# Block-scaled MLP stage: which engine multiplies by the inverse maxima, which adds the residual, and the order of TensorE's queue

## Chip, cores and metric

The kernel runs on one core of a Trainium2 chip. The metric is the device time of one execution in microseconds (us), as the median of several runs. Engines are named as the profile names them: PE (TensorE, matrix products; PEld its weight loads), DVE (VectorE), ACT (ScalarE), POOL (GpSimd) and SP (SyncE, which here only issues DMAs).

## What is computed

Two blocks, each an attention and a feed-forward part, on x of shape 32 x 64 x 128. The change touches only the last part, a gated MLP whose operands are quantized to FP4 in blocks of 16 along the last dimension:

```python
def fp4_quant_dequant(x):
    xb = x.reshape(shape[:-1] + (shape[-1] // 16, 16))
    scale = jnp.maximum(jnp.max(jnp.abs(xb), axis=-1, keepdims=True) / 6.0, 1e-12)
    xn = xb / scale
    idx = jnp.searchsorted(_MID, jnp.abs(xn))        # nearest of 0, .5, 1, 1.5, 2, 3, 4, 6
    return (_GRID[idx] * jnp.sign(xn) * scale).reshape(shape)

gate = fp4_linear(x, w_gate)          # 128 -> 352, both operands quantized
y    = fp4_linear(x, w_up)            # 128 -> 352
h    = silu(gate) * y
out  = residual + g * fp4_linear(h, w_down)   # 352 -> 128
```

## The kernel before, in words

The 2048 tokens are 16 tiles of 128 tokens. The MLP works on pairs of tiles: `PAIRS` is 8, `WHOLE` is 6 (pairs 0 to 5 are handled whole), and the last two pairs are finished in `LAST` = 4 halves. There is no planner: every engine's order is written out by hand, and each engine runs its own queue in that order. A `wait_ge` holds up everything behind it in the same queue.

For one pair q of h the steps are these.

- PE `gate(q)` and `up(q)` multiply the quantized x by the two weights into PSUM (L1599). ACT `silu(q)` (L721) writes silu(gate) to `sg`.
- DVE `pair_step(q)`: the product h = silu * up into `hh` (L1090, one input in PSUM), the maximum of each block of 16 into `hmx` (L1095, 44 maxima for each token row), their reciprocals `hin` (L1101), and `fp4_shrunk` (L286), which multiplies h in place by a constant and by the reciprocal of its block, spread over the 16 elements. That is 128 x 704 elements, and it counts `hv_done`.
- ACT `magnitude(q)` (L728) writes |h| times a constant to `hm`. DVE rounds in two steps (`fp4_off`, L294, both inputs in SBUF) into `hd`. In the queue this stands in `pair_step(q+1)`, right behind L286 of pair q+1, so it is the pair before that is rounded.
- POOL `h_scale(q)` (L290) turns the maxima into scales, and `fp4_unscale` (L301) multiplies `hd` by them, 128 x 704, into `hq`. For the last four halves DVE does this itself (`round_half`, L301 on 128 x 352).
- PE `turn_h(q)` transposes `hq` (L1625), ACT copies the result to `hT` (L775), PE `down(q)` multiplies by the down weights (L1636). `down` first adds the residual on PE, as a product of the identity with x (L1631), and ACT `finish(q)` copies the sum into x (L755) and counts `x4_done`. SP stores the pair.

The x of the MLP is quantized in the same way, in four groups of four tiles: `x_scale` (L281, L282, L286) and `x_round` (L294) on DVE, `x_unscale` (L290, L301 on 128 x 512) on POOL. Groups 2 and 3 of these stand between the steps of pairs 0 to 3.

PE's order for iteration q of the loop is `up(q+1)`, `turn_h(q-2)`, `down(q-2)`, `gate(q+2)`. ACT's is `silu(q+1)`, `finish(q-3)`, the copy of `hT` for pair q-2, `magnitude(q)`.

Of the kernel before, what the change touches and what calls it, by code (L numbers as in the profile page):

```python
# [15 lines left out]
ALU = mybir.AluOpType  # L16
# [10 lines left out]
MT = 3  # L27
# [75 lines left out]
def build(nc, a):  # L103
    with ExitStack() as ctx:
# [21 lines left out]
        def carve(start, *shape):  # L126
            return shaped(region[:, start:start + int(np.prod(shape))], shape)
# [62 lines left out]
        hb = [carve(8576 + 2 * NH * (BLK + 1) * i, 2 * NH, BLK + 1) for i in range(2)]  # L190
        xb = carve(21952, TILES * D // BLK, BLK + 1)
        hm, hd = ([carve(k + 2 * MLP * i, 2 * MLP) for i in range(2)] for k in range(12 * MLP, 20 * MLP, 4 * MLP))
        hT = [carve(7040 + 2 * MT * P * i, 2, MT, P) for i in range(2)]

        stats, mv, ve, rstd = sm(TILES, 6), sm(TILES, 2), sm(TILES), sm(TILES)
# [26 lines left out]
        x2_tr x2_done xn_c xn_c_late xn_c_dve xf_done xf_used q_done pp_done hs_done hs_read hs_turned cf_ready corr_done corr_read  # L222
        dve_c lead_ready lead_exp lags_ready lags_turned gx_ready g_done of_done of_ready
        y1_done y1_ready o_done x3_read x3_done
        floors_set hsc_ready xsc_ready rolled_made codes_set xn_d xv_done xm_done xd_done xq_done xqt_done xqt_used gate_done gu_done sg_done hh_done hv_done hm_done hd_done hq_done hq_last ht_done ht_used dn_done x4_done out_done dve_d""".split()
        m = {n: ctx.enter_context(nc.semaphore(n)) for n in names}
        x_sem = [m["ld_x0"], m["ld_x1"]]
        w_sem = [m[f"w{i}"] for i in range(6)]
# [55 lines left out]
        def fp4_shrunk(eng, out, src, inv):  # L284

            return eng.scalar_tensor_tensor(out, src, 6.0 / FINE * (1.0 - 2.0 ** -24), inv, ALU.mult, ALU.mult)  # L286
# [13 lines left out]
        def fp4_unscale(eng, diff, sc, nblk, out):  # L300
            return eng.tensor_tensor(blocks(out), blocks(diff), spread(sc, nblk), ALU.mult)  # L301


        @block.sync
        def _(sp):
            xs = a["x"].rearrange("(t u) s d -> (u s) t d", u=2)
            sp.dma_start(par[:, 0:NPAR_K], a["par"][:, 0:NPAR_K]).then_inc(m["ld_wk"], 16)
            sp.dma_start(ctxS[:, 0:8 * S], a["ctxT"][:, 0:8 * S]).then_inc(m["ld_ctx0"], 16)
            sp.dma_start(par[:, NPAR_K:NPAR_A], a["par"][:, NPAR_K:NPAR_A]).then_inc(m["ld_par"], 16)
            sp.dma_start(ctxS[:, 8 * S:16 * S], a["ctxT"][:, 8 * S:16 * S]).then_inc(m["ld_ctx1"], 16)  # L310
            sp.dma_start(x[:, 0:TILES // 2, :], xs[:, 0:TILES // 2, :]).then_inc(m["ld_x0"], 16)
            sp.dma_start(ctxS[:, 16 * S:B * S], a["ctxT"][:, 16 * S:B * S]).then_inc(m["ld_ctx2"], 16)
            sp.dma_start(x[:, TILES // 2:TILES, :], xs[:, TILES // 2:TILES, :]).then_inc(m["ld_x1"], 16)
            sp.dma_start(par[:, NPAR_A:NPAR], a["par"][:, NPAR_A:NPAR]).then_inc(m["ld_rest"], 16)
            sp.dma_start(ctxN[:], a["ctx"].rearrange("(t u) s d -> (u s) t d", u=2)).then_inc(m["ld_ctxn"], 16)
            for e in range(E):
                sp.dma_start(wall[:, e, :], a["wall"][e]).then_inc(m["ld_wall"], 16)
            sp.wait_ge(m["x1_done"], TILES)
            sp.dma_start(wnat, a["ffn"]).then_inc(m["ld_ffn"], 16)
            sp.wait_ge(m["ld_wall"], 16 * E)  # L320
            sp.wait_ge(m["experts_ready"], 1)

            def feed(j):

                e = sp.value_load(experts[0:1, j:j + 1], min_val=0, max_val=E - 1)
                if j >= 6:
                    sp.wait_ge(m["y2_done"], j - 5)
                sp.dma_start(wbuf[j % 6], wall[:, bass.ds(e, 1), :].rearrange("p a w -> p (a w)")).then_inc(w_sem[j % 6], 16)

            for j in range(MOE_TILES):  # L330
                feed(j)
            out = a["out"].rearrange("(q t u) s d -> q (u s) t d", t=2, u=2)
            for q in range(WHOLE):
                sp.wait_ge(m["x4_done"], q + 1)
                sp.dma_start(out[q], x[:, 2 * q:2 * q + 2, :]).then_inc(m["out_done"], 16)
            for n in range(LAST):
                sp.wait_ge(m["x4_done"], WHOLE + n + 1)
                q, t = WHOLE + n // 2, n % 2
                sp.dma_start(out[q][:, t:t + 1, :], x[:, 2 * q + t:2 * q + t + 1, :]).then_inc(m["out_done"], 16)
            sp.wait_ge(m["out_done"], 16 * (WHOLE + LAST))  # L340
# [3 lines left out]
        def _(pool):  # L344
# [142 lines left out]
            x_unscale(1)  # L487
            def h_scale(q):

                pool.wait_ge(m["hv_done"], q + 1)  # L490
                if q >= 3:
                    pool.wait_ge(m["hq_done"], q - 2)
                fp4_scale(pool, hmx[q % 3], hsc[q % 3]).then_inc(m["hsc_ready"], 1)

            for q in range(1, WHOLE + 1):
                u = (q - 1) % 2
                if q in (1, 3):
                    x_unscale((q + 3) // 2)
                h_scale(q - 1)
                pool.wait_ge(m["hd_done"], q)  # L500
                pool.wait_ge(m["hsc_ready"], q)
                if q >= 3:
                    pool.wait_ge(m["ht_done"], q - 2)
                fp4_unscale(pool, hd[u], hsc[(q - 1) % 3], 2 * NH, hq[u].rearrange("p a n -> p (a n)")).then_inc(m["hq_done"], 1)
            for q in range(WHOLE, PAIRS):
                h_scale(q)


        @block.scalar
        def _(act):  # L510
# [241 lines left out]
            normalise(act, 12, 16, m["xn_d"], 14, blocked=True)  # L752
            def finish(q):
                act.wait_ge(m["dn_done"], q + 1)
                act.copy(x[:, 2 * q:2 * q + 2, :].rearrange("p t d -> p (t d)"), ps[:, 7, 0:2 * D]).then_inc(m["x4_done"], 1)  # L755

            def half_turned(n):
                p, t = WHOLE + n // 2, n % 2
# [2 lines left out]

            def half_finish(n):
                act.wait_ge(m["dn_done"], WHOLE + n + 1)
                act.copy(x[:, 2 * WHOLE + n, :], ps[:, 1 + n, 0:D]).then_inc(m["x4_done"], 1)

            for q in range(PAIRS):
                if q + 1 < PAIRS:
# [23 lines left out]
        def _(dve):  # L791
# [291 lines left out]
            def pair_step(q):  # L1083

                u, w, n3 = q % 2, (q - 1) % 2, q % 3
                if q < PAIRS:
                    dve.wait_ge(m["sg_done"], q + 1)
                    dve.wait_ge(m["gu_done"], q + 1)
                    rows = "p a (n k) -> p a n k"
                    dve.tensor_tensor(hh[u].rearrange("p (a n) k -> p a n k", a=2), sg[u].rearrange(rows, k=BLK),  # L1090
                                      ps[:, 3:5, 0:MLP].rearrange(rows, k=BLK), ALU.mult).then_inc(m["hh_done"], 1)
                    if q >= 3:
                        dve.wait_ge(m["hq_done"], q - 2)
                    dve.wait_ge(m["hh_done"], q + 1)
                    k = dd.mark(dve.tensor_reduce(hmx[n3], hb[u], AX, ALU.max, apply_absolute_value=True))  # L1095
                    if q in (1, 3):
                        x_round((q + 3) // 2)
                    if q == 2:
                        x_scale(3)
                    dd.after(k)  # L1100
                    dd.step(dve.reciprocal(hin[n3], hmx[n3]))  # L1101
                    fp4_shrunk(dve, hh[u], hh[u], spread(hin[n3], 2 * NH)).then_inc(m["hv_done"], 1)
                    if q == 0:
                        x_scale(2)
                if 1 <= q <= WHOLE:
                    dve.wait_ge(m["hm_done"], q)
                    if q >= 3:
                        dve.wait_ge(m["hq_done"], q - 2)
                    dd.step(fp4_off(dve, blocks(hd[w]), blocks(hm[w]), hh[w]))
                    fp4_off(dve, hd[w], hm[w], hd[w]).then_inc(m["hd_done"], 1)  # L1110
# [29 lines left out]
        def _(pe):  # L1140
# [486 lines left out]

            def down(q):
                if q:
                    pe.wait_ge(m["x4_done"], q)  # L1630
                mm(ps[:, 7, 0:2 * D], ident, x[:, 2 * q:2 * q + 2, :].rearrange("p t d -> p (t d)"), start=True, stop=False)  # L1631
                pe.wait_ge(m["ht_used"], q + 1)
                for t in range(2):
                    for k in range(MT):
                        n = min(P, MLP - P * k)
                        ins = mm(ps[:, 7, D * t:D * t + D], hT[q % 2][0:n, t, k, :], wdT[0:n, k, :],  # L1636
                             start=False, stop=(t == 1 and k == MT - 1))
                ins.then_inc(m["dn_done"], 1)

            def turn_half(n):  # L1640
# [26 lines left out]
            for q in range(PAIRS):  # L1667
                if q + 1 < PAIRS:
                    up(q + 1)
                if q >= 2:  # L1670
                    turn_h(q - 2)
                    down(q - 2)
                if q == 0:
                    turn_x(1)
                if q + 2 < PAIRS:
                    gate(q + 2)
                if q in (1, 3):
                    turn_x((q + 3) // 2)
            turn_half(0)
# [121 lines left out]
```

## Time and profile before

| | us |
|---|---|
| median of 3 runs | 275.0 (274.87 to 275.17) |
| profiled execution, first to last instruction | 274.8 |
| MLP pair steps on DVE (L1090 of pair 0 to the last L301) | 221.16 to 270.44 |
| behind the last DVE instruction | 4.4 |

All times below are counted from the span's start. A row of a timeline has the start, the duration, the engine, the line, the operation, what it writes and reads, shapes, and "xN" where N like instructions are merged; in brackets stands how long the engine was idle before it and what ended that. An instruction's duration includes the time for which it is held up after its start, so a duration above the usual one of the same shape shows that something stood in its way. On DVE an instruction can start a little before the one ahead of it has ended.

### The profile page before, as it was taken

The numbers are of one execution on the slowest core, as the hardware profiler recorded it, in microseconds if no ns is written. First come the engines' busy times: TensorE is split into PE (matmuls) and PEld (weight loads), VectorE is DVE, ScalarE is ACT, GpSimd is POOL, SyncE is SP. The second block draws the span as 40 slices with busy tenths as digits, with TensorE's granted clock in tenths as the row PEclk, the third lists the DMA queues.
The fourth block names the chain that finished last, engine by engine and source line by source line (L and its number), as shares of the span: only waits on it lengthen the run. The fifth ranks groups of instructions, "written<-read, shape, count | busy, mean of one in ns | idle before, by whom it ended". The sixth has DMA issues, their size and how long they took to land.

```text
span 274.8 us, 6251 instructions
## 1 busy us (share of the span) xinstructions
PE 253.9 (92%) x2152; PEld 196.4 (71%) x2152; DVE 190.7 (69%) x494; ACT 164.6 (60%) x384; POOL 131.0 (48%) x207
## 2 busy tenths in 40 slices
PE   8999999999899989999999999979998784989886
PEld 6655376666577868999999999665785442766675
DVE  3898688888988763253222223885769989999993
ACT  2369985666488654675566667473445793354453
POOL 4566579999402403218992220275066633353230
PEclk9999999999999998999999999999999999799999
DMA  6999000000000209776777771000000000000111
GB/s 191 379 348 403 13 4 2 2 4 0 2 2 4 76 20 377 300 289 265 296 300 291 292 290 63 2 1 1 4 0 0 0 0 2 0 19 23 38 39 38
DMA packets 12191, 30.11 MB, mean 110 GB/s; under 512 B 1024, under 2 KB 5248, under 8 KB 12032
## 3 DMA queue, kind: packets, MB, share of 16 engines
q1 hardware_dynamic: 12160, 29.71, 28.5%
q8 instruction: 17, 0.28, 0.4%
q14 instruction: 14, 0.11, 0.1%
HBM read 9.71 MB, written 1.05 MB: 39 GB/s over the span
## 4 chain that ended last, share of the span: by engine, by line
PE 64%; DVE 20%; issue 7%; ACT 5%; POOL 2%; DVEq 0%; POOLq 0%
PE ps L1403 12%; PE ps L1414 12%; PE ps L1252 6%; DVE s_region L294 4%; PE ps L1226 4%; PE ps L1239 4%; PE ps L1159 3%; DVE s_region L1090 3%; PE ps L1542 3%; PE ps L1150 2%; DVE s_small L1095 2%; PE ps L1262 2%; PE ps L1151 2%; PE ps L1344 2%; DVE s_small L237 2%
## 5 line engine op out<-in xcount | busy, mean ns | idle before, releaser
L631 ACT ACTIVATE s_region<-ps,s_region 128x128 f32<-128x128 f32 x144 | 40.8, 371 | 21.8 <-PE ps L1403 21.8
L960 DVE SCALAR_TENSOR_TENSOR s_ctxT<-ps,s_region,s_ctxT 128x64 f32 x72 | 18.1, 281 | 43.8 <-PE ps L1414 43.8
L1403 PE MATMUL ps<-s_region 128*128 128x128 f32 x288 | 38.0, 276 | 0.3 <-issue 0.3
L1414 PE MATMUL ps<-s_region 128*128 128x128 f32 x288 | 37.9, 275 | 0.0
L1403 PEld LDWEIGHTS ps<-s_region 128*128 128x128 f32 x288 | 34.9, 192 | 0.7 <-issue 0.7
L1414 PEld LDWEIGHTS ps<-s_region 128*128 128x128 f32 x288 | 35.0, 192 | 0.2 <-issue 0.2
L420 POOL COPY s_region<-s_xt 128x64 f32 x72 | 14.8, 234 | 32.3 <-PE ps L1403 24.5
L574 ACT COPY s_region<-ps 128x512 f32<-128x512 f32 x32 | 17.2, 592 | 16.2 <-PE ps L1239 16.2
L830 DVE TENSOR_REDUCE s_small<-ps 128x16 f32<-128x1024 f32 x16 | 19.6, 1224 | 9.7 <-PE ps L1226 9.7
L1599 PE MATMUL ps<-s_region 128*128 128x352 f32 x64 | 21.1, 469 | 5.3 <-DVE s_region L1090 3.7
L301 POOL TENSOR_TENSOR s_region<-s_region,s_small 128x704 f32<-128x704 f32 (+2 forms) x11 | 14.6, 1330 | 22.0 <-DVE s_region L294 21.7
L364 POOL TENSOR_SCALAR s_region<-s_region 128x512 f32<-128x512 f32 x16 | 24.7, 1569 | 0.0
L267 POOL TENSOR_SCALAR s_small<-s_small 128x4 f32<-128x4 f32 (+3 forms) x14 | 3.2, 232 | 40.8 <-DVE s_small L244 40.8
L294 DVE SCALAR_TENSOR_TENSOR s_region<-s_region 128x704 f32<-128x704 f32 (+2 forms) x28 | 20.4, 728 | 0.5
L1599 PEld LDWEIGHTS ps<-s_region 128*128 128x128 f32 x64 | 11.3, 189 | 11.9 <-DVE s_region L1090 5.2
L838 DVE TENSOR_TENSOR s_region<-ps,s_small 128x1024 f32<-128x1024 f32 x16 | 18.7, 1170 | 0.1
L1252 PE MATMUL ps<-s_region 128*64 128x18 f32 x512 | 17.8, 212 | 0.8 <-ACT s_region L574 0.7
L1252 PEld LDWEIGHTS ps<-s_region 128*64 128x64 f32 x512 | 16.3, 138 | 3.0 <-ACT s_region L574 1.4
L569 ACT ACTIVATE s_region<-s_region 128x1024 f32<-128x1024 f32 x16 | 17.2, 1073 | 1.1 <-DVE s_region L838 1.1
L1226 PE MATMUL ps<-s_region 64*64 64x512 f32 x128 | 17.4, 615 | 0.0
L1239 PE MATMUL ps<-s_par,s_region 128*128 128x128 f32 x128 | 16.7, 273 | 0.0
L269 POOL TENSOR_TENSOR s_small<-s_small,s_par 128x4 f32<-128x4 f32 (+3 forms) x14 | 16.7, 1191 | 0.0
(230 smaller groups left out, 528.7 us busy)
## 6 DMA issues: line engine op xcount, KB each, us to landing
s_region<-s_wall SPq DMA_DIRECT2D x36, 514.0 KB, 3.0
s_wall<-wall SPq DMA_DIRECT2D x8, 514.0 KB, 9.3
s_par<-par SPq DMA_DIRECT2D x1, 1280.0 KB, 10.5
s_x<-x SPq DMA_DIRECT2D x2, 512.0 KB, 6.8
out<-s_x SPq DMA_DIRECT2D x6, 128.0 KB, 1.8
s_region<-ffn SPq DMA_DIRECT2D x1, 560.0 KB, 3.6
s_ctxT<-ctxT SPq DMA_DIRECT2D x2, 256.0 KB, 4.0
s_ctxT<-ctxT SPq DMA_DIRECT2D x1, 512.0 KB, 6.7
```

What stands on the lines that cost most here:

```text
L294: return eng.scalar_tensor_tensor(out, mag, 1.5, z, ALU.max, ALU.subtract)
L364: pool.tensor_scalar(kbd[g % 2][:, j, :], cols, hmask[:, j:j + 1], None, ALU.mult).then_inc(m["kbd_done"], 1)
L631: ins = act.activation(hg[j % 3][:, c, :], ps[:, j % 3, RPT * S * c:RPT * S * (c + 1)], ACT.Gelu, bias=wbuf[j % 6][:, FF + FC * D + c:FF + ...
L830: dve.tensor_reduce(mx[t % 2], scores(t % 2), AX, ALU.max).then_inc(m["mx_done"], 1)
L838: dve.tensor_tensor(ssub[t % 2], scores(t % 2), mx[t % 2].unsqueeze(2).broadcast_to([P, H, S]), ALU.subtract).then_inc(m["s_sub"], 1)
L960: dve.scalar_tensor_tensor(row, ps[:, 4 + j % 2, S * k:S * k + S], w, row, ALU.mult, ALU.add).then_inc(m["acc_done"], 1)
L1226: ins = mm(ps[S * row:S * row + S, 2 * (t % 2) + half, :], qT[rows, 2 * t + row, :], kbd[g % 2][rows, :, k:k + S], start=True, stop=True)
L1239: ins = tr(ps[:, 4 + half, P * k:P * k + P], pr[t % 2][:, c:c + P], ident)
L1252: ins = mm(ps[S * row:S * row + S, 6 + t % 2, n * c:n * c + n], pT[t % 2][:, c, S * row:S * row + S], vbd[:, 2 * t + row, c, :], start=Tru ...
L1403: ins = mm(ps[:, j % 3, RPT * S * c:RPT * S * (c + 1)], w[:, P * c:P * c + P], xg[j % 4], start=True, stop=True)
L1414: ins = mm(ps[:, 4 + j % 2, 0:RPT * S], w[:, FF + D * c:FF + D * c + D], hg[j % 3][:, c, :], start=(c == 0), stop=(c == FC - 1))
L1599: ins = mm(ps[:, 1 + 2 * n + t, 0:MLP], xqT[(q // 2) % 2][:, lo:lo + P], wguT[:, MT * P * n:MT * P * n + MLP], start=True, stop=True)
```

## The change

The multiplication by the reciprocal leaves DVE: DVE scales the 44 reciprocals of a row by the constant (a small `tensor_scalar`), and POOL multiplies h by them (`h_shrunk`). The residual is no longer added by PE but by POOL (`residual`), from a copy of the down product that ACT writes to a new buffer `yT`. In PE's queue `gate(q+2)` now stands ahead of `down(q-2)`. The last four halves keep their residual on PE, with a semaphore of their own.

```diff
+        yT = [carve(26880 + 2 * D * i, 2 * D) for i in range(2)]
@@ SP
             for n in range(LAST):
-                sp.wait_ge(m["x4_done"], WHOLE + n + 1)
+                sp.wait_ge(m["x4_half"], n + 1)
@@ POOL
             def h_scale(q):
-                pool.wait_ge(m["hv_done"], q + 1)
+                pool.wait_ge(m["hin_ready"], q + 1)
...
-            for q in range(1, WHOLE + 1):
-                u = (q - 1) % 2
+            def h_shrunk(q):
+                pool.wait_ge(m["hin_ready"], q + 1)
+                pool.wait_ge(m["hh_done"], q + 1)
+                pool.tensor_tensor(hh[q % 2], hh[q % 2], spread(hin[q % 3], 2 * NH), ALU.mult).then_inc(m["hv_done"], 1)
+            def h_unscale(q):
...
+            def residual(q):
+                pool.wait_ge(m["dn_copied"], q + 1)
+                pair = x[:, 2 * q:2 * q + 2, :].rearrange("p t d -> p (t d)")
+                pool.tensor_tensor(pair, pair, yT[q % 2], ALU.add).then_inc(m["x4_done"], 1)
+            for q in range(PAIRS):
                 if q in (1, 3):
                     x_unscale((q + 3) // 2)
-                h_scale(q - 1)
...
-            for q in range(WHOLE, PAIRS):
+                h_shrunk(q)
                 h_scale(q)
+                if 1 <= q <= WHOLE:
+                    h_unscale(q - 1)
+                if q >= 4:
+                    residual(q - 4)
+            residual(WHOLE - 2)
+            residual(WHOLE - 1)
@@ ACT
             def finish(q):
                 act.wait_ge(m["dn_done"], q + 1)
-                act.copy(x[:, 2 * q:2 * q + 2, :].rearrange("p t d -> p (t d)"), ps[:, 7, 0:2 * D]).then_inc(m["x4_done"], 1)
+                if q >= 2:
+                    act.wait_ge(m["x4_done"], q - 1)
+                act.copy(yT[q % 2], ps[:, 7, 0:2 * D]).then_inc(m["dn_copied"], 1)
@@ DVE
                     dd.step(dve.reciprocal(hin[n3], hmx[n3]))
-                    fp4_shrunk(dve, hh[u], hh[u], spread(hin[n3], 2 * NH)).then_inc(m["hv_done"], 1)
+                    dve.tensor_scalar(hin[n3], hin[n3], 6.0 / FINE * (1.0 - 2.0 ** -24), None, ALU.mult).then_inc(m["hin_ready"], 1)
@@ PE
             def down(q):
                 if q:
-                    pe.wait_ge(m["x4_done"], q)
-                mm(ps[:, 7, 0:2 * D], ident, x[:, 2 * q:2 * q + 2, :].rearrange("p t d -> p (t d)"), start=True, stop=False)
+                    pe.wait_ge(m["dn_copied"], q)
...
                 if q >= 2:
                     turn_h(q - 2)
-                    down(q - 2)
                 if q == 0:
                     turn_x(1)
                 if q + 2 < PAIRS:
                     gate(q + 2)
+                if q >= 2:
+                    down(q - 2)
```

## Rows read from the trace of the kernel before

**Rows 1.** Page, busy us, share of the span and instructions by engine
```profile
PE 253.9 (92%) x2152; PEld 196.4 (71%) x2152; DVE 190.7 (69%) x494; ACT 164.6 (60%) x384; POOL 131.0 (48%) x207
```

**Rows 2.** Busy us by engine, 5 us stretch: PE, PEld, DVE, ACT, POOL, PEclk, DMA
```profile
251.00:256.00 5.00, 4.55 (x26) 3.25 (x25) 4.79 (x8) 2.35 (x4) 1.70 (x2) 1.00 0.11 31
```

**Rows 3.** All waits of DVE from 221.2 to 271: total, times, longest
```profile
DVE s_region L1090 <- PE ps L1599: 0.8, 1, 0.8
```

**Rows 4.** Timeline of DVE, pair 6, to the start of pair 7
```profile
255.97 0.88 DVE L1090 TENSOR_TENSOR s_region<-s_region,ps 128x704 f32<-128x704 f32 x1
256.95 0.93 DVE L1095 TENSOR_REDUCE s_small<-s_region 128x44 f32<-128x748 f32 x1
257.92 0.43 DVE L1101 RECIPROCAL s_small<-s_small 128x44 f32<-128x44 f32 x1
258.38 0.89 DVE L286 SCALAR_TENSOR_TENSOR s_region<-s_region,s_small 128x704 f32<-128x704 f32 x1
259.19 1.81 DVE L294 SCALAR_TENSOR_TENSOR s_region<-s_region 128x704 f32<-128x704 f32 x2
260.91 0.88 DVE L1090 TENSOR_TENSOR s_region<-s_region,ps 128x704 f32<-128x704 f32 x1
```

**Rows 5.** Timeline of POOL in the same stretch
```profile
256.13 1.39 POOL L301 TENSOR_TENSOR s_region<-s_region,s_small 128x704 f32<-128x704 f32 x1 [3.16 <-DVE s_region L294]
257.60 0.32 POOL L290 TENSOR_SCALAR s_small<-s_small 128x44 f32<-128x44 f32 x1
```

**Rows 6.** Timelines of POOL and DVE, pair 1, from 229.3
```profile
229.31 1.06 POOL L301 TENSOR_TENSOR s_region<-s_region,s_small 128x512 f32<-128x512 f32 x1 [2.79 <-DVE s_region L294]
230.45 0.84 POOL L290 TENSOR_SCALAR s_small<-s_small 128x44 f32<-128x44 f32 x1
229.60 1.51 DVE L286 SCALAR_TENSOR_TENSOR s_region<-s_region,s_small 128x704 f32<-128x704 f32 x1
```

**Rows 7.** Timelines early in the kernel; last row: L372's min/median/max in ns
```profile
16.56 0.87 DVE L816 TENSOR_SCALAR s_region<-s_region 128x512 f32<-128x512 f32 x2
17.46 1.50 POOL L372 TENSOR_TENSOR s_region<-s_region 128x512 f32<-128x512 f32 x1
17.75 1.50 DVE L816 TENSOR_SCALAR s_region<-s_region 128x512 f32<-128x512 f32 x1
...
L372 POOL TENSOR_TENSOR s_region<-s_region x6: 1268/1273/1502, 9.2 to 26.3; 128x512 f32<-128x512 f32 x6
```

**Rows 8.** Timelines of DVE and POOL at the first half
```profile
264.13 0.52 DVE L294 SCALAR_TENSOR_TENSOR s_region<-s_region 128x352 f32<-128x352 f32 x1
264.30 0.53 POOL L290 TENSOR_SCALAR s_small<-s_small 128x44 f32<-128x44 f32 x1 [1.43 <-DVE s_region L286]
264.69 0.53 DVE L294 SCALAR_TENSOR_TENSOR s_region<-s_region 128x352 f32<-128x352 f32 x1
```

**Rows 9.** Nearest rows for new instructions: L466's min/median/max in ns, DVE timeline
```profile
L466 POOL TENSOR_TENSOR s_region<-s_region x8: 723/728/730, 199.0 to 208.9; 128x256 f32<-128x256 f32 x8
...
218.82 0.17 DVE L247 TENSOR_SCALAR s_small<-s_small 128x4 f32<-128x4 f32 x1
218.92 0.69 DVE L294 SCALAR_TENSOR_TENSOR s_region<-s_region 128x512 f32<-128x512 f32 x1
```

**Rows 10.** Timelines of PE and ACT around pair 6
```profile
255.52 1.60 PE L1636 MATMUL ps<-s_region 128*128 128x128 f32 x12 [0.45 <-ACT s_region L775]
256.96 2.53 PE L1599 MATMUL ps<-s_region 128*128 128x352 f32 x8
...
255.36 0.79 ACT L728 ACTIVATE s_region<-s_region 128x704 f32<-128x704 f32 x1
```

**Rows 11.** Timeline of DVE, pair 0 and the x group behind it
```profile
223.50 0.89 DVE L286 SCALAR_TENSOR_TENSOR s_region<-s_region,s_small 128x704 f32<-128x704 f32 x1
...
225.44 0.69 DVE L286 SCALAR_TENSOR_TENSOR s_region<-s_region,s_small 128x512 f32<-128x512 f32 x1
```

**Rows 12.** Timeline of DVE, its last instruction
```profile
269.91 0.53 DVE L301 TENSOR_TENSOR s_region<-s_region,s_small 128x352 f32<-128x352 f32 x1
```

More of the change, by code:

```diff
@@ L224, in build @@
         y1_done y1_ready o_done x3_read x3_done
-        floors_set hsc_ready xsc_ready rolled_made codes_set xn_d xv_done xm_done xd_done xq_done xqt_done xqt_used gate_done gu_done sg_done hh_done hv_done hm_done hd_done hq_done hq_last ht_done ht_used dn_done x4_done out_done dve_d""".split()
+        floors_set hsc_ready xsc_ready rolled_made codes_set xn_d xv_done xm_done xd_done xq_done xqt_done xqt_used gate_done gu_done sg_done hh_done hin_ready hv_done hm_done hd_done hq_done hq_last ht_done ht_used dn_done dn_copied x4_half x4_done out_done dve_d""".split()
         m = {n: ctx.enter_context(nc.semaphore(n)) for n in names}
@@ L493, in h_scale @@
                 fp4_scale(pool, hmx[q % 3], hsc[q % 3]).then_inc(m["hsc_ready"], 1)
-            for q in range(1, WHOLE + 1):
-                u = (q - 1) % 2
+            def h_shrunk(q):
[3 more added lines that the diff above has]
+            def h_unscale(q):
+                pool.wait_ge(m["hd_done"], q + 1)
+                pool.wait_ge(m["hsc_ready"], q + 1)
+                if q >= 2:
+                    pool.wait_ge(m["ht_done"], q - 1)
+                fp4_unscale(pool, hd[q % 2], hsc[q % 3], 2 * NH, hq[q % 2].rearrange("p a n -> p (a n)")).then_inc(m["hq_done"], 1)
+            def residual(q):
[3 more added lines that the diff above has]
+            for q in range(PAIRS):
                 if q in (1, 3):
                     x_unscale((q + 3) // 2)
-                h_scale(q - 1)
[L500 to L504, printed above, removed]
-            for q in range(WHOLE, PAIRS):
-                h_scale(q)
+                h_shrunk(q)
+                h_scale(q)
+                if 1 <= q <= WHOLE:
[4 more added lines that the diff above has]
+            residual(WHOLE - 1)
         @block.scalar
@@ L763, in half_finish @@
                 act.wait_ge(m["dn_done"], WHOLE + n + 1)
-                act.copy(x[:, 2 * WHOLE + n, :], ps[:, 1 + n, 0:D]).then_inc(m["x4_done"], 1)
+                act.copy(x[:, 2 * WHOLE + n, :], ps[:, 1 + n, 0:D]).then_inc(m["x4_half"], 1)
             for q in range(PAIRS):
@@ L1636, in down @@
                         ins = mm(ps[:, 7, D * t:D * t + D], hT[q % 2][0:n, t, k, :], wdT[0:n, k, :],
-                             start=False, stop=(t == 1 and k == MT - 1))
+                             start=(k == 0), stop=(k == MT - 1))
                 ins.then_inc(m["dn_done"], 1)
@@ L1676, in _ @@
                     gate(q + 2)
+                if q >= 2:
+                    down(q - 2)
                 if q in (1, 3):
```

## Prediction

> **What bounds the kernel now.** I read the busy shares first. PE is busy 92% of the span and DVE 69% [rows 1], but that is a mean over stages, and the change lies in the last 54 us only. So the second view is the busy time of a 5 us stretch inside the MLP: there DVE is busy 4.79 of 5.00 us, PE 4.55, POOL 1.70 [rows 2]. The third is DVE's list of waits: from 221.2 us to its last instruction it waits once, for 0.8 us, at pair 0 [rows 3]. An engine that never waits is the bound of its stage, so the stage is worth what DVE's queue adds up to. DVE's timeline gives one pair: L1090 at 0, L1095 at +0.98, L1101 at +1.95, L286 at +2.41, the two rounding steps L294 at +3.22, the next L1090 at +4.94 [rows 4]. POOL's timeline shows one 1.39 us product and one small instruction in that time [rows 5]. DVE's last instruction ends at 270.44 [rows 12], and 4.4 us of PE, ACT and the last store follow in the span of 274.8. I leave these as they are.
>
> **One thing more has to be read: when POOL and DVE collide.** In one pair the POOL product (256.13 to 257.52) lies beside L1090 and L1095, and all three keep their usual durations [rows 4, 5]: L1090 has one input in PSUM, L1095 has one input. In pair 1 a POOL product (to 230.37) meets L286, which has two inputs in SBUF [rows 6]. L286 takes 1.51 instead of 0.89 and ends 0.74 after the POOL product's end; the product keeps its usual 1.06. So DVE stood still until POOL was through, with 0.15 of its 0.89 done before. There the small POOL instruction L290 takes 0.84 instead of 0.32 and ends 0.18 after L286 (231.11) [rows 6]. So POOL stands still for DVE as well, with 0.14 done before. The stage has three such collisions; one is shown.
>
> Who goes next when both want to is the question on which this change hangs. Early in the kernel four like DVE instructions L816 follow each other without a wait, 0.48 us each at a pitch of 0.40. A POOL product L372 starts at 17.46 inside the third (which ends at about 17.83) and ends at 18.96, that is 1.13 after 17.83 where it usually takes 1.27 in all; the fourth L816, started at 17.75, takes 1.50 and ends 0.29 after POOL [rows 7]. POOL, once waiting, went ahead of DVE's next instruction. At the first half a small POOL instruction does the same between the two L294: it ends at 264.83, 0.18 after the first L294 and long before the end of the second [rows 8].
>
> **Part 1: L286 becomes a small scaling on DVE.** Its price on DVE is a pitch. Nearest row: the small scaling L247 is followed 0.10 later by the next instruction and lasts 0.17 [rows 9]. The other end is the small L1101, 0.46 to the next [rows 4], but that is a reciprocal with a wait behind it. I take 0.11 and a duration of 0.19 for 44 elements. L286's pitch was 0.81 [rows 4]. Gain: 0.70 a pair.
>
> **Part 2: the product on POOL.** It has L301's shape, a 128x704 operand and 44 values spread over 16, so 1.39 [rows 5]. If two full operands were the better likeness, 0.73 for 256 elements and 1.27 for 512 [rows 7, 9] give 2.1 ns an element and 1.68; that is my upper end. I find no row for a lower price than 1.39. The scaled reciprocals are ready at +2.60. At +2.52 DVE has already begun the first L294 of the pair before, both of whose inputs are in SBUF. POOL's product therefore waits until +3.41, goes next [rows 7, 8], and ends at 3.41 + (1.39 - 0.14) = +4.66. The second L294 stands still until then and ends 0.74 later, at +5.40. Without the product it would have ended at +4.33. So the product costs DVE 1.07 a pair, against a gain of 0.70. The pitch of a pair becomes 5.40 - 0.09 = 5.31 or 5.32, where it was 4.94: **+0.38 a pair**.
>
> The Trainium skill speaks against this change: SBUF — State Buffer, section "Who interferes with whom", says that a VectorE instruction with two SBUF inputs contends with a GpSimd instruction that reads SBUF, and that the one which issued first keeps the shared ports for its whole length. By that rule the product blocks L294 as the row shows it for L286 [rows 6], and the sum is the same. GPSIMD Engine Reference, section "Elementwise — side-by-side cycle accounting", puts a two-input product at about 2.6 cycles of 1.2 GHz an element; my estimate from it is 1.53 for 704 elements, and the sum would be about 1.1 higher. The row has 1.39 [rows 5], and I use that.
>
> **Part 3: the rest of POOL's queue.** Behind the product stand `h_scale`, the unscaling product and, from iteration 4, an addition. The scale waits for the second L294 and ends at +5.58 (0.18 after it [rows 6]). The unscaling product runs from +5.66 to +7.05, that is beside the next L1090 and L1095, where it costs nothing now [rows 4, 5]. The addition of 256 elements, 0.73 by its nearest row with two full operands [rows 9], ends at +7.86. The next pair's small scaling on DVE wants its turn at about 5.32 + 2.41 + 0.14 = +7.87. So additions 0 to 2 cost nothing, by a hair: each 0.1 that POOL is later costs 0.1, for three pairs. Additions 3 to 5 come in iteration 7 and behind the loop, where DVE does only the halves, twelve instructions with two SBUF inputs each. There each addition holds DVE up by 0.59 less the 0.06 to 0.17 that DVE needs anyway to its next instruction: 0.53 + 0.42 + 0.42 = 1.37. The lower end is 0, were they to find a gap.
>
> **Part 4: PE and ACT.** The identity product leaves PE, and `gate` fills the 0.45 that PE waits for the copy of hT [rows 10]. This is worth nothing while DVE is the bound: `up(7)` ends at 259.49, and DVE takes its result at 260.91 [rows 4, 10]. That slack of 1.4 is the cover, and it grows with a longer pair. New waits: `finish(q-3)` on ACT waits for addition q-5, which ends at about +2.5 of iteration q. The hT copy and `magnitude(q)` stand behind it; `magnitude(q)` can't start before the product's end at +4.66, so the two copies, under 1.2 together, fit ahead of it. `magnitude` then ends at about 4.66 + 0.79 = +5.5 [rows 10], and its reader, L294 in the next iteration, begins at +7.84: 2.3 to spare. SP's stores of whole pairs wait for the additions; the last one comes about 2 us before the first half is ready, so the halves' stores are not held up.
>
> **The sum.** Pair 0 has no L294 behind it. Its product starts at about 223.8 and ends at about 225.17; L286 of the x group, moved forward from 225.44 to 224.74, is held until then and ends at 225.72 instead of 226.13 [rows 11]: -0.41. Pairs 1 to 6: 6 x 0.38 = +2.28; the two old collisions among them (L286 behind the x unscaling, about 0.6 each) stay, since the small scaling meets the same POOL product. Pair 7 and the halves: -0.70, +1.08 for its product against a half's second step, +1.37 for three additions: +1.75. Together +3.6. The profiled span of 274.8 becomes 278.4; it is 0.2 under the median of the runs, so the median becomes **278.6**. Own range of this forecast: 276.9 (additions 3 to 5 hidden, some tenths of pitch) to 280.9 (product at 1.68: 8 x 0.29 = 2.3 more).
>
> **Rivals.**
> - *Faster: DVE keeps its turn through both rounding steps.* The second L294 follows the first by 0.03. If it starts before POOL gets in, POOL's product waits to +4.33 and runs beside L1090 and L1095. It decides as soon as the product costs DVE less than the 0.70 that L286 cost. Then pair 0 gives -0.41, pairs 1 to 6 give -4.2, and pair 7 about 0: near 270.4. If POOL and DVE didn't collide here at all, the old collisions would go too, some 1.9 more: 267.5 to 268. For it: the gap is short. Against: POOL got in every time [rows 6 to 8], once where DVE's next instruction had already started. Chance 0.12.
> - *Slower still: POOL is the bound.* Its pair has 1.39 + 0.32 + 1.39 + 0.73 plus three gaps and its waits, and it is through only at +7.86. A product at 1.68 and a small scaling near the reciprocal's 0.46 (0.35 x 8) would give 281 to 284. For it: no slack is left in POOL's loop. Against: nearly the same shapes have prices [rows 5, 9]. Chance 0.10.
> - *No change that can be told.* The product's wait halves by some offset between the engines, 0.7 against 0.7, and the additions find gaps: 274.5 to 275.5. Nothing in the rows points there. Chance 0.05.
> - *It doesn't do what it says:* DVE's queue doesn't get shorter because `magnitude` comes late over three engines. 2.3 us of slack speak against it; I put it within the last rival.
>
> **How the numbers follow.** The forecast has 0.73. A measurement of this kernel can tell about 0.2%, 0.55 us, from no change. Slower: 0.73 + 0.10 = 0.83; within 0.2%: 0.05; faster: 0.12. The range holds the forecast, no change's upper half and most of the slower rival: 275.0 to 281.9. It leaves out the faster rival and a part of the others, under 0.2 in all.
>
> **What would show it.** In the profile after: no L286 of 704 elements on DVE; the first L294 of a pair at its usual 0.89 and the second near 2.0 (beginning +3.44, ending +5.40); a pitch of L1090 of 5.3 us in pairs 4 to 6; POOL's product near 2.0 long, since it starts behind DVE, and its unscaling at 1.39; three halves' instructions near 0.95 to 1.1 instead of 0.52. Wrong it would be if the second L294 stays at 0.89, if the pitch falls to about 4.2 to 4.7, or if L1090 shows new idle time behind PE.

## The result and the profile after

| | before | after |
|---|---|---|
| median, us | 274.96 (274.87 to 275.17) | 279.94 (279.05 to 282.54) |
| profiled execution, span, us | 274.8 | 277.9 |
| first MLP pair's L1090 to DVE's last instruction, us | 49.28 | 52.72 |
| of it, pitches of that product (pair 0 to 1, 1 to 2, ...), us | 4.90 6.73 6.49 6.80 4.95 4.95 4.94 | 4.47 7.06 6.85 7.13 5.30 5.31 5.30 |
| of it, from pair 7's L1090 on, us | 9.52 | 11.31 |

The changed kernel takes 1.0187 of the time before (95% interval 1.0137 to 1.0236): slower, as forecast. A second series, shown below, gives 1.0112 (1.0030 to 1.0193). Executions of one kernel spread: in the later series the kernel before took 274.6 to 282.0 us, with medians of 276.5 to 277.3, so the four executions in the table lie at its low end, and the 5.0 us between the two medians is more than the 3.44 that the trace puts down to the changed stage.

Lines have moved in the changed kernel: L1112 is the gated product (L1090 before), L1117 the maxima, L1123 the reciprocal, L1124 the new small scaling, L295 the rounding steps, L302 POOL's unscaling, L500 POOL's product and L514 POOL's addition. DVE's timeline for pair 6, as in [rows 4]; in the first fence the two rounding steps are merged, in the second the step at 255.06 is the second one of the pair ahead, and the step at 259.44 the first one of this pair:

```profile
256.94 0.87 DVE L1112 TENSOR_TENSOR s_region<-s_region,ps 128x704 f32<-128x704 f32 x1
257.92 0.93 DVE L1117 TENSOR_REDUCE s_small<-s_region 128x44 f32<-128x748 f32 x1
258.88 0.43 DVE L1123 RECIPROCAL s_small<-s_small 128x44 f32<-128x44 f32 x1
259.34 0.19 DVE L1124 TENSOR_SCALAR s_small<-s_small 128x44 f32<-128x44 f32 x1
259.44 2.88 DVE L295 SCALAR_TENSOR_TENSOR s_region<-s_region 128x704 f32<-128x704 f32 x2
262.24 0.87 DVE L1112 TENSOR_TENSOR s_region<-s_region,ps 128x704 f32<-128x704 f32 x1
```

```profile
255.06 1.96 DVE L295 SCALAR_TENSOR_TENSOR s_region<-s_region 128x704 f32<-128x704 f32 x1
...
259.44 0.88 DVE L295 SCALAR_TENSOR_TENSOR s_region<-s_region 128x704 f32<-128x704 f32 x1
```

And POOL's timeline beside it, as in [rows 5]:

```profile
259.61 1.96 POOL L500 TENSOR_TENSOR s_region<-s_region,s_small 128x704 f32<-128x704 f32 x1 [0.26 <-DVE s_small L1124]
261.65 0.84 POOL L291 TENSOR_SCALAR s_small<-s_small 128x44 f32<-128x44 f32 x1
262.58 1.39 POOL L302 TENSOR_TENSOR s_region<-s_region,s_small 128x704 f32<-128x704 f32 x1
263.92 0.73 POOL L514 TENSOR_TENSOR s_x<-s_x,s_region 128x256 f32<-128x256 f32 x1
```

Read the two together. POOL starts its product at 259.61, inside DVE's first rounding step (259.44 to 260.32). It ends at 261.57, which is 1.25 after that step's end, and its record is 1.96 long instead of 1.39. DVE's second rounding step starts at about 260.36 and ends at 262.32, 0.75 after POOL's product. L291 then waits for that step and ends about 0.17 after it. Unscaling and addition run beside L1112, L1117 and L1123 at their usual lengths and cost DVE nothing; the addition ends at 264.65, and the next small scaling begins at 264.64.

The halves, DVE first and then POOL (two of the three additions are merged in one row):

```profile
264.74 2.15 DVE L295 SCALAR_TENSOR_TENSOR s_region<-s_region 128x352 f32<-128x352 f32 x2
266.92 0.53 DVE L302 TENSOR_TENSOR s_region<-s_region,s_small 128x352 f32<-128x352 f32 x1
267.37 2.02 DVE L295 SCALAR_TENSOR_TENSOR s_region<-s_region 128x352 f32<-128x352 f32 x2
269.42 1.02 DVE L302 TENSOR_TENSOR s_region<-s_region,s_small 128x352 f32<-128x352 f32 x1
```

```profile
264.91 1.59 POOL L500 TENSOR_TENSOR s_region<-s_region,s_small 128x704 f32<-128x704 f32 x1 [0.26 <-DVE s_small L1124]
...
267.15 1.85 POOL L514 TENSOR_TENSOR s_x<-s_x,s_region 128x256 f32<-128x256 f32 x2
269.34 0.72 POOL L514 TENSOR_TENSOR s_x<-s_x,s_region 128x256 f32<-128x256 f32 x1 [0.34 <-ACT s_region L777]
```

Two rounding steps of a half take 1.08 alone. The product makes the first two 2.15, two additions make the next two 2.02, and the third addition makes an L302 of 0.52 into 1.02. After these, everything is at its usual length again.

DVE's waits between 220.85 and its end, all of them, and the busy times of the stretch of the pair steps in both kernels (columns as in [rows 2]; first the kernel before, then the changed one):

```profile
DVE s_region L1112 <- PE ps L1621: 0.8, 1, 0.8
```

```profile
221.16:270.44 49.28, 40.78 (x217) 29.53 (x215) 47.52 (x66) 24.58 (x45) 15.90 (x20) 0.97 0.06 18
```

```profile
220.83:273.55 52.72, 41.59 (x204) 31.07 (x203) 50.96 (x66) 24.03 (x44) 38.20 (x34) 0.87 0.06 16
```

DVE waits for PE as little as before [rows 3]. PE's granted clock in this stretch was 0.87 of full speed on average against 0.97, so PE worked at its lower level (1.2 GHz) for longer; DVE's only wait for PE is still the 0.8 at pair 0, so this cost the stretch nothing. POOL is busy for 38 us where it was 16, but a busy share counts the time in which an instruction is held up: of the pair shown, 0.57 of the product's 1.96 and about 0.5 of L291's 0.84 are waiting. ACT does wait for POOL now, as the row of its copy of pair 4 shows:

```profile
264.74 0.37 ACT L777 COPY s_region<-ps 128x256 f32<-128x256 f32 x1 [2.34 <-POOL s_x L514]
```

Nobody was held up by that: what stands behind it, `magnitude(7)`, needs the product that ends at 266.50.

### The profile page after: what moved, and what is told of

The parts are those of the page before. It is cut to its first block, busy times and chain, and to the rows that moved or that the text cites. A ratio compares the mean times of both kernels' runs of the same rounds, so it can differ in the third digit from the quotient of the medians.

```text
span 277.9 us, 6258 instructions
## 1 busy us (share of the span) xinstructions
PE 254.3 (91%) x2140; PEld 197.9 (71%) x2140; DVE 194.2 (70%) x494; ACT 164.6 (59%) x384; POOL 153.3 (55%) x221
## 4 chain that ended last, share of the span: by engine, by line
PE 63%; DVE 20%; issue 8%; ACT 5%; POOL 2%; DMA 1%; SPq 0%; DVEq 0%; POOLq 0%
PE ps L1425 12%; PE ps L1436 12%; PE ps L1274 6%; DVE s_region L295 4%; PE ps L1248 4%; PE ps L1261 4%; PE ps L1181 3%; DVE s_region L1112 3%; PE ps L1564 3%; DVE s_small L1117 2%; PE ps L1172 2%; PE ps L1284 2%; PE ps L1173 2%; PE ps L1366 2%; DVE s_small L238 2%
## 5 line engine op out<-in xcount | busy, mean ns | idle before, releaser
L1621 PE MATMUL ps<-s_region 128*128 128x352 f32 x64 | 24.0, 510 | 7.3 <-DVE s_region L1112 5.7
L295 DVE SCALAR_TENSOR_TENSOR s_region<-s_region 128x704 f32<-128x704 f32 (+2 forms) x28 | 28.7, 1026 | 0.5
L500 POOL TENSOR_TENSOR s_region<-s_region,s_small 128x704 f32<-128x704 f32 x8 | 14.7, 1842 | 5.9 <-DVE s_small L1124 5.6
L302 POOL TENSOR_TENSOR s_region<-s_region,s_small 128x704 f32<-128x704 f32 (+2 forms) x11 | 14.6, 1330 | 4.1 <-DVE s_region L295 3.3
```

What stands on the lines that cost most here:

```text
L295: return eng.scalar_tensor_tensor(out, mag, 1.5, z, ALU.max, ALU.subtract)
L1621: ins = mm(ps[:, 1 + 2 * n + t, 0:MLP], xqT[(q // 2) % 2][:, lo:lo + P], wguT[:, MT * P * n:MT * P * n + MLP], start=True, stop=True)
```

## Experiments

The theory to test: POOL and DVE exclude each other where POOL reads SBUF and DVE has two inputs there, or runs a `tensor_scalar` from SBUF such as L816 in [rows 7]; POOL, once waiting, goes ahead of DVE's next instruction; so the product costs DVE 1.07 a pair against 0.70 gained, and additions cost only beside the halves. Rivals: the additions or PE's order make the loss; any POOL instruction at that place does; or the loss is PE's lower clock. "The stretch" below is the time from pair 0's gated product to DVE's last instruction; it is taken from the trace, and the two profiled executions of the changed kernel agree in it within 0.02 us. Each ratio is to executions of the kernel before in the same series.

**Product alone.** Residual and PE's order as before.

```diff
-                    fp4_shrunk(dve, hh[u], hh[u], spread(hin[n3], 2 * NH)).then_inc(m["hv_done"], 1)
+                    dve.tensor_scalar(hin[n3], hin[n3], 6.0 / FINE * (1.0 - 2.0 ** -24), None, ALU.mult).then_inc(m["hin_ready"], 1)
@@ POOL
+                pool.tensor_tensor(hh[q % 2], hh[q % 2], spread(hin[q % 3], 2 * NH), ALU.mult).then_inc(m["hv_done"], 1)
```

> Only the product with the scaled reciprocals is on POOL; residual and PE's order as before. Theory (POOL and DVE exclude each other where both read SBUF, and POOL goes next): pitch of DVE's L1090-like product 5.3 us in pairs 4 to 7 (before 4.95), second rounding step near 1.95 us, stretch of the pair steps on DVE 2.1 us longer than before; time about 277.1. Rival (the additions and PE's new order make the loss, the product is hidden behind the gain of 0.7 a pair): pitch 4.3 to 4.9, time 275 or less.

Measured: 1.0074 of before (1.0031 to 1.0118); stretch 51.29, +2.01; pitch 5.30 to 5.31 in pairs 4 to 7; second rounding step 1.96. All as the theory had it.

**Addition alone.** Product on DVE, PE's order as before.

```diff
-                act.copy(x[:, 2 * q:2 * q + 2, :].rearrange("p t d -> p (t d)"), ps[:, 7, 0:2 * D]).then_inc(m["x4_done"], 1)
+                act.copy(yT[q % 2], ps[:, 7, 0:2 * D]).then_inc(m["dn_copied"], 1)
@@ POOL
+                pool.tensor_tensor(pair, pair, yT[q % 2], ALU.add).then_inc(m["x4_done"], 1)
```

> Only the residual's addition is on POOL (from the buffer that ACT writes); product on DVE and PE's order as before. Theory: pitch 4.95 as before, additions 0 to 2 hidden at 0.73 us, additions 3 to 5 beside the halves cost 0.53 + 0.42 + 0.42; time about 276.2 to 276.4. Rival (additions are late enough or find gaps): 275.0.

Measured: 1.0063 (1.0009 to 1.0116); stretch 50.58, +1.30; pitch 4.95. Of POOL's timeline, an addition inside the pairs and the three beside the halves:

```profile
261.49 0.73 POOL L508 TENSOR_TENSOR s_x<-s_x,s_region 128x256 f32<-128x256 f32 x1
...
263.98 2.82 POOL L508 TENSOR_TENSOR s_x<-s_x,s_region 128x256 f32<-128x256 f32 x3
```

The addition inside is at its own 0.73; the three at the end take 2.82 together, since each waits for a step of DVE, and DVE for each of them.

**PE's order alone.**

```diff
                     turn_h(q - 2)
-                    down(q - 2)
...
                     gate(q + 2)
+                if q >= 2:
+                    down(q - 2)
```

> Only PE's order is changed: gate of pair q+2 ahead of the down product of pair q-2. Theory: DVE is the bound and has 1.4 us of slack on PE at pair 7, so no change: 274.7 to 275.3. Rival (PE's order matters, through the halves or the clock): a change of over 0.6 us either way.

Measured: 0.9975 (0.9927 to 1.0023); stretch 49.30, +0.02. No change that can be told, and DVE's list of waits is the same one entry of 0.8.

The three parts give +2.01 + 1.30 + 0.02 = +3.33 in the stretch, all of them together +3.44. The 0.1 between them lies behind pair 7's gated product, where the additions cost 1.34 alone and 1.44 on top of the product.

**Late additions on PE.** The changed kernel, with the residual of pairs 3 to 5 added by the identity product as before.

```diff
+                late = q >= 3
+                if late:
+                    mm(ps[:, 7, 0:2 * D], ident, x[:, 2 * q:2 * q + 2, :].rearrange("p t d -> p (t d)"), start=True, stop=False)
@@ POOL
-                if q >= 4:
+                if 4 <= q < 7:
                     residual(q - 4)
-            residual(WHOLE - 2)
-            residual(WHOLE - 1)
```

> The changed kernel, but the residual of pairs 3 to 5 is added on PE as before; additions 0 to 2 stay on POOL. Theory: the three additions beside the halves cost 1.4 us of DVE; without them the stretch of the pair steps is 1.4 us shorter than in the changed kernel, and the halves' instructions are at 0.52 except the one that the last product holds up. Rival (they cost little, and the loss in the halves is all the product's): under 0.5 us shorter.

Measured: 1.0085 (1.0049 to 1.0120); stretch 51.31, which is 1.41 less than in the changed kernel and within 0.02 of the product alone. So additions 0 to 2 are free and 3 to 5 cost 1.4.

**A fill in place of the product.** What is left out: the multiplication of h by the reciprocals.

```diff
-                pool.tensor_tensor(hh[q % 2], hh[q % 2], spread(hin[q % 3], 2 * NH), ALU.mult).then_inc(m["hv_done"], 1)
+                pool.memset(hh[q % 2], 0.01).then_inc(m["hv_done"], 1)
```

> The changed kernel with POOL's product replaced by a fill of the same 128 x 704 elements with a constant, so the multiplication is left out: POOL writes but reads nothing there. Theory (the collision is over reading SBUF): the second rounding step is back at 0.89 us, pitch of pairs 4 to 6 near 4.3 (or what PE then allows, up to 4.7). Rival (any POOL instruction of that length holds DVE up): the second rounding step stays above 1.2 us and the pitch above 4.7.

DVE's and POOL's timelines for pair 5:

```profile
249.52 0.19 DVE L1124 TENSOR_SCALAR s_small<-s_small 128x44 f32<-128x44 f32 x1
249.62 1.81 DVE L295 SCALAR_TENSOR_TENSOR s_region<-s_region 128x704 f32<-128x704 f32 x2
251.35 0.88 DVE L1112 TENSOR_TENSOR s_region<-s_region,ps 128x704 f32<-128x704 f32 x1
```

```profile
249.77 0.69 POOL L500 MEMSET s_region<- 128x704 f32 x1 [0.23 <-DVE s_small L1124]
250.54 1.08 POOL L291 TENSOR_SCALAR s_small<-s_small 128x44 f32<-128x44 f32 x1
```

The fill writes as many elements to the same place and starts at the same point of the pair, 0.15 behind the first rounding step's start. Neither side waits: 0.69 on POOL, 1.81 for both steps on DVE, a pitch of 4.24 and a stretch of 44.93. As this fill is through (250.46) before the second step starts (250.54), the pair alone shows only that the fill doesn't wait for DVE. That DVE doesn't wait for the fill is seen in pair 7, where the steps are those of a half:

```profile
258.10 1.07 DVE L295 SCALAR_TENSOR_TENSOR s_region<-s_region 128x352 f32<-128x352 f32 x2
...
258.25 0.69 POOL L500 MEMSET s_region<- 128x704 f32 x1 [0.23 <-DVE s_small L1124]
```

There the fill is still writing (to 258.94) when the second step starts (258.65), and the two steps take their usual 1.07. So it isn't the place in the queue, the semaphores or POOL's writing. What the product has and the fill lacks is the reading of SBUF (and the multiplication itself, which this run doesn't tell apart from it). L291, which reads, waits as before. It starts at the same 250.54 as the second step, and here DVE goes first: L291 ends 0.19 after that step. POOL goes ahead of DVE's next instruction where it was waiting already.

**The product behind both rounding steps.** Only the product on POOL, with one wait more.

```diff
                 pool.wait_ge(m["hh_done"], q + 1)
+                if 1 <= q <= WHOLE:
+                    pool.wait_ge(m["hd_done"], q)
```

> Only the product on POOL (residual and PE's order as before), and it waits until both rounding steps of the pair before are done. Theory (the two engines share one way of reading): both rounding steps back at 0.89 us and the product at 1.39 beside the next pair's first step; but POOL's unscaling is pushed from there to 2.0 to 3.4 us of the pair, and the small scaling on DVE now waits for it until about 3.4: pitch 5.0 to 5.1, stretch of the pair steps 49.9 to 50.1 us. So the collision moves and the gain doesn't come: 275.2 to 276. Rival (only the place of the product was bad): pitch 4.3 to 4.6 and 272 to 273.

DVE's and POOL's timelines of one pair, and all of DVE's waits:

```profile
251.05 1.14 DVE L1114 TENSOR_SCALAR s_small<-s_small 128x44 f32<-128x44 f32 x1
252.11 1.81 DVE L295 SCALAR_TENSOR_TENSOR s_region<-s_region 128x704 f32<-128x704 f32 x2
```

```profile
248.90 1.39 POOL L502 TENSOR_TENSOR s_region<-s_region,s_small 128x704 f32<-128x704 f32 x1 [1.93 <-DVE s_region L295]
250.36 0.32 POOL L291 TENSOR_SCALAR s_small<-s_small 128x44 f32<-128x44 f32 x1
250.77 1.39 POOL L302 TENSOR_TENSOR s_region<-s_region,s_small 128x704 f32<-128x704 f32 x1
```

```profile
DVE s_region L295 <- ACT s_region L746: 1.1, 1, 1.1
DVE s_region L1102 <- PE ps L1611: 0.8, 1, 0.8
```

The collision moved as expected: the product and both rounding steps are at their usual lengths, and now the small scaling on DVE, of 44 elements, takes 1.14 because it waits for the unscaling (which ends at 252.16). The pitch is 5.19 to 5.20, and the stretch 50.73, where 49.9 to 50.1 was expected: a miss. Two things that the expectation didn't have are 0.1 a pair of pitch, and a wait of 1.1 in pair 3 for ACT's magnitude of the x group, which stands behind the magnitude of the delayed product in ACT's queue. They don't settle the miss between them: the part from pair 7's gated product on took 1.3 more than in the kernel before and pairs 1 and 2 took 0.7 and 0.2 less, and the expectation gives no parts to set these against. Time: 1.0022 (0.9969 to 1.0074). Another place for the product gave back 0.56 of the 2.01 that it cost alone.

**The theory used the other way round.** The kernel before, with two of its own collisions taken out (the x unscaling against L286, [rows 6] and its like in pair 3), and the product on POOL only for pair 0, behind which no rounding step stands. POOL's `h_scale` moves ahead of the x unscaling with it.

```diff
-                    if q in (1, 3):
-                        x_round((q + 3) // 2)
...
                     fp4_off(dve, hd[w], hm[w], hd[w]).then_inc(m["hd_done"], 1)
+                if q in (1, 3):
+                    x_round((q + 3) // 2)
@@ POOL
+                if q == 1:
+                    pool.wait_ge(m["hin_ready"], 1)
+                    pool.tensor_tensor(hh[0], hh[0], spread(hin[0], 2 * NH), ALU.mult).then_inc(m["hv_first"], 1)
+                h_scale(q - 1)
                 if q in (1, 3):
                     x_unscale((q + 3) // 2)
-                h_scale(q - 1)
```

> The kernel before, with the theory used the other way round: the rounding of x groups 2 and 3 stands behind the pair's own rounding steps, so that POOL's x unscaling runs beside the next pair's first step instead of holding up L286, and only pair 0, behind which no rounding step stands, has its product on POOL. Theory: the two L286 of 1.5 us fall to 0.89 (-0.6 each, less about 0.3 that pairs 2 and 4 wait longer for POOL), pair 0 gives -0.4: stretch of the pair steps 47.8 to 48.4 us against 49.28, time 1.0 to 1.4 us under before. Rival (x groups then come too late for PE and DVE waits for gate and up): no gain, with idle time of DVE behind PE.

Measured: 0.9927 (0.9889 to 0.9964), faster than both kernels; stretch 48.18, -1.10. Pair 0 gave -0.43, pairs 1 and 3 gave -0.52 and -0.51. The loss expected in pairs 2 and 4 hardly came (0.00 and +0.04), and one that was not expected did (+0.32 between pairs 6 and 7), so that the total lies in the expected range is in part luck. L286 of pair 1 is back at 0.89 where it was 1.51 [rows 6], and DVE's waits show a small new one, 0.23 for PE ahead of pair 7:

```profile
227.91 0.89 DVE L286 SCALAR_TENSOR_TENSOR s_region<-s_region,s_small 128x704 f32<-128x704 f32 x1
...
259.76 0.89 DVE L1093 TENSOR_TENSOR s_region<-s_region,ps 128x704 f32<-128x704 f32 x1 [0.23 <-PE ps L1605]
```

**And PE's order on top of it.** The diff of PE's order alone, added to the kernel just shown.

> The kernel with the collisions taken out, and PE's order of the change on top: gate of pair q+2 ahead of the down product of pair q-2. In the kernel without that order DVE waited 0.23 us for PE before pair 7, the slack of PE being used up by DVE's shorter pairs. Theory: that wait goes, the stretch of the pair steps is 47.9 to 48.0 us against 48.18, so the order that was worth nothing alone is worth about 0.2 us here; time 1.2 to 1.5 us under the kernel before. Rival (no slack was used up, the wait has another cause): stretch 48.18 unchanged.

Measured: 0.9924 (0.9885 to 0.9962); stretch 47.84, 0.34 less and a little under the 47.9 to 48.0 expected; the wait ahead of pair 7 is gone, and DVE's only wait is pair 0's 0.8. In time the two can't be told apart; in the trace PE's order is now worth 0.3 us, where alone it was worth nothing.

**The changed kernel again.**

> The changed kernel once more, to tell its loss from what runs scatter. Theory: its loss is the 3.4 us that the pair steps on DVE take longer (52.7 against 49.3), so about 1.012 of the kernel before. Rival (the shorter-running PE work also brings lower granted clock where it costs): 1.016 or more, with more half-clock stretches and time lost outside the pair steps.

Measured: 1.0112 (1.0030 to 1.0193); stretch 52.74 (52.72 in the first profile). What differs between the two profiles lies ahead of the MLP. A stretch of 25 us in the middle of the kernel, long before any changed line (columns as above; the kernel before, the changed kernel's first and second profile, and the addition alone):

```profile
90.00:115.00 25.00, 23.72 (x204) 20.90 (x201) 13.40 (x59) 13.97 (x37) 6.74 (x28) 0.93 0.49 191
```

```profile
90.00:115.00 25.00, 23.72 (x199) 20.96 (x196) 13.19 (x58) 13.84 (x38) 6.74 (x28) 0.93 0.50 192
```

```profile
90.00:115.00 25.00, 23.72 (x175) 20.70 (x172) 12.33 (x54) 12.18 (x31) 6.16 (x26) 0.80 0.40 152
```

```profile
90.00:115.00 25.00, 23.47 (x214) 21.15 (x215) 13.79 (x60) 15.08 (x42) 7.15 (x30) 1.00 0.51 197
```

At a mean granted clock of 1.00, 0.93 and 0.80 the profile has 214, 204 and 175 products of PE in the same 25 us: PE is busy for 23.5 to 23.7 of them, and at 0.93 and 0.80 it works at its lower level for a part of them. Pair 0's gated product begins at 220.3, 221.2 and 224.0 us in these profiles (addition alone, before, changed kernel again), and at 220.8 in the changed kernel's first. This moves an execution by some us, before any changed line has run; the stretch tells the kernels apart where times of a few executions hardly do. Part of the rival has come with it: the second profile does have more time at the lower clock and time lost outside the pair steps, while the series' 1.0112 lies under its 1.016. The first profile has no more of either ahead of the MLP than the kernel before, and no run shows that the change brings it.

## Why the prediction was right, step by step

*The bound.* Right. DVE's queue set the stage before and after, with the same single wait of 0.8 [rows 3].

*Who goes next.* Right, and this carried the sign. In the changed kernel POOL's product goes ahead of the second rounding step in every pair behind which one stands, as in [rows 7, 8]. The fill, which only writes, holds nothing up. What collides was named too narrowly, though: "two inputs in SBUF" leaves out L816 in the prediction's own [rows 7], which has one input and was held up. The small scaling, with one input too, was held up by POOL's x unscaling in pairs 1 and 3 (0.81 instead of 0.19):

```profile
228.84 0.81 DVE L1124 TENSOR_SCALAR s_small<-s_small 128x44 f32<-128x44 f32 x1
```

The sum was not hurt by it, since it had put these two old collisions down as staying.

*The pair.* Forecast 5.31 to 5.32, measured 5.30 to 5.31. The small scaling was put at a pitch of 0.11 and 0.19 long, and is 0.10 and 0.19; the product's end was put at +4.66 of the pair and came at +4.63 (261.57 less 256.94); the second step's end at +5.40 came at +5.38. The end of the addition inside the pair was put at the very start of the next small scaling, and there it is (264.65 against 264.64).

*The sum of the stretch.* Forecast +3.6, measured +3.44:

| | forecast | measured |
|---|---|---|
| pair 0 | -0.41 | -0.43 |
| pairs 1 to 6 | +2.28 | +2.08 |
| pair 7 and the halves | +1.75 | +1.79 |

The pairs 1 to 3 came at +0.33 to +0.36 and 4 to 6 at +0.35 to +0.36 instead of +0.38 each; the first rounding step began at +2.50 and ended at +3.38 of the pair, where +2.52 and +3.41 were forecast, and the product went with it. Nothing else was off by more than 0.05. For the halves alone, 1.37 was put on three additions; the experiment without them gives 1.41.

*Nothing for PE and ACT.* Right for the changed kernel: PE's order alone +0.02, and ACT's new waits for POOL of up to 2.3 us cost nothing. The slack of 1.4 us that covered it is real, too: once DVE's pairs up to pair 6 were shortened by 1.4 in all, 0.23 of a wait for PE appeared ahead of pair 7, and PE's new order removed it.

*From the span to the median.* Here a step was wrong. The prediction took the profiled span of 274.8 to stand 0.2 under its own time. In every run listed with both, the time is 1.8 above the span (279.76 and 277.9 for the changed kernel's profiled run). By an estimate from this, the profiled execution of before took about 276.6, 1.6 longer than the median of the four; that is where the medians of the later series lie. As the sum is a difference, the forecast of +3.6 wasn't touched by this; but it was added to a base that was 1.6 low, and of the measured +5.0 in the medians only 3.4 is in the stretch of the change. From 276.6 the same sum would give 280.2, beside the measured 279.94. The second series, with 1.0112 or about +3.1, agrees with the stretch. The lower mean clock of the changed kernel's four executions (0.957 to 0.981) doesn't explain the other 1.5: its profiled execution has 0.969 against 0.988 for the one of before, at the same 0.93 from 90 to 115 us, and the difference of 0.02 is what the clock of 0.87 against 0.97 in the stretch makes of the mean, where it costs nothing. Whether the change lengthens some executions beyond what the two profiles show stays open: the shortest of its ten took 278.97, 4.4 more than the shortest of the kernel before.

*The rivals.* The faster one (DVE keeps its turn through both steps) is out: no pair shows it. No change is out as well, with the stretch 3.44 longer in both profiles. The slower one (POOL is the bound) didn't come, though it was close: POOL ends its addition within 0.01 of the point from which it would have cost.

By the Trainium skill, SBUF — State Buffer, section "Who interferes with whom", a GpSimd instruction that only writes doesn't contend with a VectorE instruction with two SBUF inputs. The fill agrees: 0.69 beside a rounding step of its usual length. The same section of the Trainium skill says that `tensor_scalar`, which has one input, can contend as well, when it enters a mode that uses both ports. No row here names the mode; the small scaling of 1.14 behind POOL's unscaling agrees that it contends.

## What to carry to other kernels

Before work is moved from VectorE to GpSimd, look in the trace for places where the two have met already: a record longer than its like, ending a fixed time after the other engine's, is a turn taken, and it prices the move. Ask then not only how long the moved instruction is, but beside which instructions it will run; here 1.39 us of product cost 1.07 beside a step with two SBUF inputs, and the same length of unscaling cost nothing beside the product with an input in PSUM and beside the maxima. One input is no safe sign: the small `tensor_scalar` of 0.19 took 1.14 when the unscaling stood in its way. The same reading, used on collisions that the kernel already had, gave the gain that the change didn't.

## What was not expected of the hardware

A GpSimd fill of 128x704 ran beside VectorE's two-input step with no wait on either side (0.69 and 0.89 us), where a product with the same output waited 0.57 and made the next step wait 1.07. And a VectorE instruction of 44 elements, 0.19 us alone, took 1.14 behind a GpSimd product of 1.39 and 0.81 behind one of 1.06. Its wait followed from how much of the other instruction was left, not from its own size.
